# Starting the FFN's first pair of batches inside attention's last two tiles, and copying V of each batch's second tile without its wait on a DMA

## What is computed

```python
for i in range(DEPTH):            # DEPTH = 6
    x = attn_layer(shift_tokens(x), Wqkv[i], q_scale[i], k_scale[i], Wo[i]) + x
    x = ffn_layer(shift_tokens(x), ln_g[i], ln_b[i], W1[i], b1[i], W2[i], b2[i]) + x
```

```python
mu = x.mean(-1, keepdims=True)
var = ((x - mu) ** 2).mean(-1, keepdims=True)
xn = (x - mu) / jnp.sqrt(var + 1e-05) * g + bln
a, gate = jnp.split(xn @ W1 + b1, 2, -1)      # 341 channels each
return a * jax.nn.gelu(gate, approximate=False) @ W2 + b2
```

## Time and profile before

| | us |
|---|---|
| runs (three) | 4357.13, 4359.65, 4364.4 |
| median | 4359.65 |
| profiled execution, its own time | 4356.64 |
| its span, first to last instruction | 4354.8 |
| PE busy | 4059.5 (93%) |
| DVE busy | 3340.9 (77%) |
| ACT busy | 2354.2 (54%) |
| POOL busy | 2615.3 (60%) |
| mean granted TensorE clock | 0.978 |

### The profile page before, as it was taken

The page is one execution under the profiler, slowest core; times in us unless marked ns, Lnnn a source line. Parts: engine busy times, 40 slices in busy tenths (PEclk is TensorE's granted clock), DMA queues, the critical chain, the costliest instruction groups (busy, mean ns, idle before and its releaser), DMA issues. The chain is left out here.

```text
span 4354.8 us, 164452 instructions
## 1 busy us (share of the span) xinstructions
PE 4059.5 (93%) x68429; PEld 2650.8 (61%) x68429; DVE 3340.9 (77%) x5657; ACT 2354.2 (54%) x3362; POOL 2615.3 (60%) x3605
## 2 busy tenths in 40 slices
PE   4988999979998999998999999999899998999998
PEld 2554333346776667765677666776657776577765
DVE  7786988758787687876878767788767877688776
ACT  3664777745554455554555544555445555455553
POOL 5462111067875478772787736878457785477871
PEclk9998999989999999999999999999999999999999
DMA  2222111133232132321323213233123322133221
GB/s 76 85 81 67 56 52 54 35 84 81 76 82 66 44 81 74 82 68 42 80 77 84 76 31 82 75 83 79 51 59 80 83 76 71 39 78 82 76 74 40
DMA packets 218146, 300.55 MB, mean 69 GB/s; under 512 B 44336, under 2 KB 112048, under 8 KB 216624
## 3 DMA queue, kind: packets, MB, share of 16 engines
q1 hardware_dynamic: 217520, 290.63, 24.9%
HBM read 60.29 MB, written 14.68 MB: 17 GB/s over the span
## 5 line engine op out<-in xcount | busy, mean ns | idle before, releaser
L1586 ACT ACTIVATE ls_r<-PS 128x1024 f32<-128x1024 f32 x192 | 196.7, 1025 | 768.5 <-PE PS L1416 742.2
L1723 DVE TENSOR_REDUCE ls_ss<-ls_r 128x16 f32<-128x1024 f32 x384 | 465.9, 1215 | 83.9 <-ACT ls_r L1624 83.9
L1713 DVE TENSOR_TENSOR ls_a<-PS,TC 128x1024 f32<-128x1024 f32 x384 | 467.8, 1220 | 65.6 <-ACT ls_r L1586 60.1
L1293 POOL TENSOR_TENSOR ls_a<-ls_a,ls_q 128x1024 f32<-128x1024 f32 x192 | 453.9, 2364 | 92.8 <-DVE ls_q L1718 91.8
L1718 DVE TENSOR_TENSOR ls_q<-PS,TS 128x512 f32<-128x512 f32 x768 | 491.6, 682 | 0.0
L1316 POOL TENSOR_TENSOR ls_a<-ls_a,ls_q 128x1024 f32<-128x1024 f32 x192 | 456.8, 2379 | 2.6 <-DVE ls_a L1713 2.6
L1624 ACT ACTIVATE ls_r<-PS 128x1024 f32<-128x1024 f32 x186 | 190.8, 1026 | 390.1 <-PE PS L1481 390.1
L1481 PE MATMUL PS<-WQ,ls_xsT 128*128 128x512 f32 x744 | 386.5, 644 | 12.9 <-ACT ls_vt L1616 12.9
L1507 PE MATMUL PS<-WO,ls_r 128*128 128x128 f32 x3072 | 396.7, 283 | 0.8 <-ACT ls_r L1628 0.8
L1313 POOL TENSOR_TENSOR ls_a<-ls_a,ls_rn 128x1024 f32<-128x1024 f32 x192 | 365.4, 1903 | 29.2 <-DVE ls_rn L1783 14.6
L1318 POOL TENSOR_TENSOR ls_a<-ls_a,ls_rn 128x1024 f32<-128x1024 f32 x192 | 365.6, 1904 | 15.1
(11 more groups left out here) (281 smaller groups left out, 8473.4 us busy)
## 6 DMA issues: line engine op xcount, KB each, us to landing
ls_vb<-ls_vt SPq DMA_DIRECT2D x1152, 130.0 KB
ls_vb<-ls_vt SPq DMA_DIRECT2D x672, 65.0 KB
QT<-scratch SPq DMA_DIRECT2D x576, 32.0 KB
KT<-scratch SPq DMA_DIRECT2D x576, 32.0 KB
WQ<-wqkv SPq DMA_DIRECT2D x7, 1536.0 KB, 6.6
ls_xs<-XL SPq DMA_DIRECT2D x42, 256.0 KB, 3.4
ls_vb<-ls_vz SPq DMA_DIRECT2D x96, 65.0 KB
scratch<-QP SPq DMA_DIRECT2D x48, 128.0 KB, 1.8
```

Of the source, the lines that this page charges most:

```text
L1293: pool.tensor_tensor(a4[:, 1], a4[:, 1], b4[:, 1], ALU.add).then_inc(s_ck, 1)
L1713: nc.vector.tensor_tensor(v4(A[fq])[:, a], src, tab, ALU.mult).then_inc(done, 1)
L1723: nc.vector.tensor_reduce(ss[:, fq, a * H:a * H + H], v4(SQ)[:, a], AX.X, ALU.add).then_inc(done, 1)
```

## The change

Three things change, in each of the six layers.

1. The last two slots now have orders of their own: 4 is the second-last slot and 5 the last one. The rows of the first FFN pair are made one slot earlier, in the second-last slot. ACT now copies their lower channels too (DVE did). DVE centres stream 0 ahead of the reciprocals and stream 1 behind the scaling of the output; ACT squares both between the copy of transposed K and the copies of the transposed output.
2. The transposes of the first pair, its gain and bias, and four of its six gate products (chunks 1 and 2 of each stream) stand in the last slot; the first pair is taken out of the FFN loop.
3. ACT copies V of a batch's second tile (t = 1) without the wait for the windows of t = 0.

```diff
                 for j in range(NT):
-                    slot(*last(j), 3 if j < NT - 1 else 4)
+                    slot(*last(j), 3 if j < 2 else j + 2)
...
             def ahead(eng, layer):
-                with loop(eng, 0, PAIRS - 1) as p:
+                layer(0, True, True)
+                with loop(eng, 1, PAIRS - 1) as p:
                     layer(p, True)
                 layer(PAIRS - 1, False)
...
+                def rows_across(s, at, m):
+                    pe.wait_ge(f_xn[s], m)
+                    for t in range(NT):
+                        ins = pe.transpose(at[:, t * P:t * P + P], xs[s][:, t, :], ident)
+                    ins.then_inc(f_xt[s], 1)
+
+                def expand(s, part, c):
+                    k = P if c < DCH - 1 else DLAST
+                    at = part * DI + c * P
+                    return pe.matmul(bank(s, 1 + c)[0:k], WA[:, at:at + k], xsT[s][:, XO:], start=True, stop=True)
...
+                        if order == 5:
+                            for s in range(2):
+                                rows_across(s, banks(2 + s), l * PAIRS + 1)
+                            pe.wait_ge(f_xe[0], l * PAIRS + 1)
+                            pe.wait_ge(f_xe[1], l * PAIRS + 1)
+                            pe.wait_ge(w_ffn, l * 64 + 64)
+                            for c in range(1, DCH):
+                                expand(0, 1, c)
...
+                            if order == 5:
+                                expand(1, 1, 1)
                             pe.wait_ge(s_pte, 2 * n)
                             pe.wait_ge(s_vb[q], windows(l, b, t))
...
+                        if order == 5:
+                            expand(1, 1, 2)
                         if back:
                             pe.wait_ge(s_y, n)
...
-                                for c in range(DCH):
-                                    k = P if c < DCH - 1 else DLAST
-                                    at = part * DI + c * P
-                                    ins = pe.matmul(bank(s, 1 + c)[0:k], WA[:, at:at + k], xsT[s][:, XO:], start=True, stop=True)
+                                for c in range(1 if begun and part else DCH):
+                                    ins = expand(s, part, c)
...
-                        if order == 4:
-                            for a in range(2):
-                                act.wait_ge(f_sh[a], l * PAIRS + 1)
-                                act.activation(xs[a][:, :, D // 2:D], banks(2 + a)[:, 0:NT * D // 2].rearrange("p (t d) -> p t d", t=NT), ACT.Copy).then_inc(f_xu[a], 1)
+                        if order == 5:
+                            for s in range(2):
+                                affine(s, banks(2 + s), l * PAIRS + 1)
                         if back:
                             for c in range(2):
                                 half = PR[:, c * T:c * T + T]
                                 act.wait_ge(s_sub, 2 * n - 1 + c)
                                 act.activation(half, half, ACT.Exp).then_inc(s_ex, 1)
+                        if order == 4:
+                            for a in range(2):
+                                act.wait_ge(f_sh[a], l * PAIRS + 1)
+                                act.activation(xs[a][:, :, 0:D // 2], XL[:, a * PAIRS, 1:SLOTS, 0:D // 2], ACT.Copy)
+                                act.activation(xs[a][:, :, D // 2:D], banks(2 + a)[:, 0:NT * D // 2].rearrange("p (t d) -> p t d", t=NT), ACT.Copy).then_inc(f_xu[a], 1)
...
                         if front:
                             act.wait_ge(s_v, nf)
-                            if order > 1:
+                            if order > 1 and ft != 1:
                                 act.wait_ge(s_vb[1 - fq], windows(l, fb, ft - 1))
...
                         if order == 4:
-                            centred(0)
+                            kf[0] = 0
+                            zeroed(0, 0, 3)
...
                         if order == 4:
+                            zeroed(0, 1)
                             rooted(0)
                             scaled(0)
```

More of the change, by code:

```diff
@@ L1516, in ready, with layer @@
                             shift(s, 0, p + s * PAIRS, f_sh[s])
-                    def layer(p, more):
+                    def layer(p, more, begun=False):
                         m = l * PAIRS + p + 1
[L1520 to L1524, removed]
+                        for s in range(0 if begun else 2):
+                            rows_across(s, bank(s, 1), m)
                         if more:
@@ L1565, in _, with affine @@
                 with loop(act, 0, DEPTH) as l:
+                    def affine(s, src, m):
+                        act.wait_ge(w_ffn, l * 64 + 64)
+                        act.wait_ge(f_xt[s], m + 1)
+                        act.activation(xsT[s][:, XO:], src, ACT.Identity, scale=COL[:, 0:1], bias=COL[:, 1:2]).then_inc(f_xe[s], 1)
                     def prep(b):
@@ L1599, in slot @@
                                 act.activation(PRT[:, c * T:c * T + T], banks(PT_BANK[c]), ACT.Copy).then_inc(s_pte, 1)
[L1600 to L1604, removed]
                         if front and order == 1:
@@ L1620, in slot @@
                             act.activation(kT[:, :, k0:k0 + P], banks(KT_BANK, 2).rearrange("p (i n) -> p i n", n=P), ACT.Copy).then_inc(s_kte, 1)
+                        if order == 4:
+                            act.wait_ge(s_rdk, (l + 1) * TILES)
+                            for a in range(2):
+                                act.wait_ge(f_c[a], l * PAIRS + 1)
+                                act.activation(XQ[a], xs[a][:, :, :], ACT.Square).then_inc(f_sq[a], 1)
                         if front and order > 1:
@@ L1639, in uppers, with layer @@
                             act.activation(xs[s][:, :, D // 2:D], bank(s, 0)[:, 0:NT * D // 2].rearrange("p (t d) -> p t d", t=NT), ACT.Copy).then_inc(f_xu[s], 1)
-                    def layer(p, more):
+                    def layer(p, more, begun=False):
                         m = l * PAIRS + p + 1
[L1643 to L1646, removed]
-                            act.activation(xsT[s][:, XO:], bank(s, 1), ACT.Identity, scale=COL[:, 0:1], bias=COL[:, 1:2]).then_inc(f_xe[s], 1)
+                        for s in range(0 if begun else 2):
+                            affine(s, bank(s, 1), m)
                         if more:
@@ L1668, in _, with flink, zeroed @@
                     spread = lambda z: z.unsqueeze(2).to_broadcast([P, NT, D])
-                    def flink(p, ins):
-                        kf[0] += 1
-                        ins.then_inc(f_ch, 1)
+                    def flink(p, ins, n=1):
+                        kf[0] += n
+                        ins.then_inc(f_ch, n)
                         dve.wait_ge(f_ch, (l * PAIRS + p) * NF + kf[0])
+                    def zeroed(p, s, n=1):
+                        dve.wait_ge(f_xu[s], l * PAIRS + p + 1)
+                        flink(p, nc.vector.tensor_reduce(fs[:, 0, s, :], xs[s][:, :, :], AX.X, ALU.add), n)
+                        flink(p, nc.vector.tensor_scalar(fs[:, 0, s, :], fs[:, 0, s, :], -1.0 / D, None, ALU.mult))
+                        nc.vector.tensor_tensor(xs[s][:, :, :], xs[s][:, :, :], spread(fs[:, 0, s, :]), ALU.add).then_inc(f_c[s], 1)
                     def centred(p):
@@ L1681, in centred @@
                         for s in range(2):
-                            dve.wait_ge(f_xu[s], m)
-                            flink(p, nc.vector.tensor_reduce(fs[:, 0, s, :], xs[s][:, :, :], AX.X, ALU.add))
-                            flink(p, nc.vector.tensor_scalar(fs[:, 0, s, :], fs[:, 0, s, :], -1.0 / D, None, ALU.mult))
-                            nc.vector.tensor_tensor(xs[s][:, :, :], xs[s][:, :, :], spread(fs[:, 0, s, :]), ALU.add).then_inc(f_c[s], 1)
+                            zeroed(p, s)
                     def rooted(p):
```

## The result

| | before | after |
|---|---|---|
| median of the runs (12 each) | 4361.74 | 4353.28 |
| lowest to highest | 4356.41 to 4371.79 | 4343.91 to 4358.47 |
| profiled execution, its own time | 4356.64 | 4351.97 |
| its span | 4354.8 | 4350.1 |
| mean granted TensorE clock | 0.978 | 0.983 |

The ratio is 0.9979, 95% interval 0.9972 to 0.9987: 9.2 us faster, by the profiled executions 4.7. The forecast was 4340, range 4329 to 4351: the direction was right, the size was not.

A forecast was written before the change was run, and what follows sets the result against it. PE was busy 93% of the span, but at the changed places engines waited for one another. V -12.9 and six layers of -0.8 (slots +0.2, first pair -1.0) took 4356.64 to 4338.9, as median 4341.9; stated 4340, range 4329 to 4351.

The forecast's parts named there:

- V of the second tile: Second slot of each layer: without ACT's wait for windows the Q product starts earlier; 12.9 us gained, bounds 7.5 and 24.3.
- all of it moves forward: Behind the Q product: ACT's square, DVE and the next scores all start earlier; 2.02 us in the second layer.
- the Q product regains its rate: Rival, second slot: the Q product runs at full rate again, up to 11.4 us more, 4329; chance 0.12.
- The slots: Attention's last two slots together, maxima to last residual: 27.86 us against a mean of 27.68, costing 0.2 a layer.
- reciprocals to maxima: From the second-last slot's reciprocals to the last slot's maxima: 8.35 us, before 7.11.
- the last slot's: Last slot, from its maxima to its reciprocals: 7.15 us, before 6.96.
- The first pair: FFN's first pair: next transposes 17.1 us after the residual, not 18.08; gain 1.0 a layer.
- some 2 us: First pair: PE stands still this long ahead of its linear products, since GELU starts only at T + 4.0 (T: the residual).
- The rule on table loads: ACT's GELU table load takes 1.28 us; whatever follows lasts 0.89 at most, against the skill's 1.38 of draining.

The follow-up runs named there:

- v_only: The kernel before with only ACT's wait at the V copy removed for the second tile; 4343.86, ratio 0.9968.
- v_unrolled: v_only with DVE's first FFN pair written ahead of its loop, no engine doing other work; 4352.84, ratio 0.9987.
- dve_loop: The changed kernel with DVE's first FFN pair back in its loop; 4337.89, ratio 0.9950.
- pad_ahead: v_only with 56 one-column memsets on DVE between attention's last slot and the FFN loop; 4366.24, ratio 1.0011.
- ffn_loop: dve_loop with ACT's wait at the V copy put back; 4359.94, ratio 1.0002.
- ffn_only: The changed kernel with ACT's wait at the V copy put back; 4356.33, ratio 0.9994.
- gates_late: dve_loop with all gate products of the first pair put back into the FFN; 4345.74, ratio 0.9971.
- tail2_pad15: The changed kernel with DVE looping over the first two FFN pairs, the last two written out, and 15 small memsets behind the last pair; 4346.32, ratio 0.9965.
- pad_behind: v_only with the same 56 memsets on DVE, placed behind the FFN loop's last pair; 4350.4, ratio 0.9975.

## Why the prediction was wrong

**V of the second tile.** The step "all of it moves forward" was right about the path and wrong about what else the change does to it. The copy, transposed K and the Q product stand as forecast. The term of 12.9 was too small rather than too large: v_only's own execution is 13.9 shorter in span though its slots and FFN happened to be 0.3 a layer longer, and its start gives 3.37 a layer, not 2.15. Of the 12.9 us of waits the first layer has only 1.0, so the five starts have 2.37 each; the other 1.03 is the rate of the Q product (2.71 us for 3.74). So the rival "the Q product regains its rate" came true by about half of its 1.9 a layer, in v_only's second layer as far as POOL allows. In the changed kernel most of that is lost again: behind DVE's gap PE waits 3.48 us, and its Q product takes 3.15 in the second layer and 3.04 in the mean.

**The step that was missing.** Nowhere did I price that the first pair is taken out of DVE's loop too, though DVE does the same in it as before. This costs 21.58 - 19.26 = 2.3 us at each of five jumps, 11.6 in all, of the 13.1 by which the profiled execution (4351.97) missed its forecast of 4338.9. v_unrolled shows it without the FFN part, dve_loop the FFN part without it, and pad_ahead with no copied pair at all. dve_loop, at 4337.89, is where the forecast had put the changed kernel, but in part by luck: V gives more there than was forecast and the FFN part less, as the sum below shows.

**The slots** were forecast at +0.2 and are +0.35 (28.27 for 27.92). Of the single steps, reciprocals to maxima is 8.17 for 8.35, the last slot's 7.45 for 7.15. The cost was right, its reason too: the residual of DVE is last, and the next maxima at 1384.11 follow it on DVE without a wait.

**The first pair** was forecast at -1.0 and gave nothing, for two reasons. Where PE's clock holds, the next transposes come 17.55 (after) to 17.66 (dve_loop) behind the residual, not 17.1: DVE's product starts at 9.9 to 10.0, not 9.65, and the FFN is 74.3 against 74.73 in four layers before, a gain of 0.4. And in five of the six layers of after the linear products run slowly behind PE's wait of 1.90 us. The clock over them, after's first layer and dve_loop's:

```profile
1402.60:1409.80 7.20, 7.12 (x14) 2.92 (x15) 5.04 (x16) 1.75 (x4) 0.98 (x1) 0.76 0.44 88
```

```profile
1402.90:1408.40 5.50, 5.42 (x12) 2.05 (x12) 4.42 (x16) 1.73 (x4) 0.96 (x1) 1.00 0.55 111
```

That is 0.8 in each such layer. The prediction had this wait of PE ("some 2 us") but put no price on the clock behind it. The wait is the same in both, so it alone doesn't decide: the slow stretch was in five layers of six in after, in one of dve_loop, in three each of ffn_loop and ffn_only. But without the wait it never came: before, v_only and gates_late, where PE runs on, have a clock of 1.00 there in all layers. Two FFNs of the kernel before are 0.6 longer all the same, at full clock; the fifth layer's, columns as above:

```profile
3692.50:3704.50 12.00, 12.00 (x33) 5.45 (x31) 10.51 (x24) 7.95 (x12) 4.08 (x4) 1.00 0.62 180
```

So the FFN part made the stretch possible; what tips it in one layer and not in another stays open.

**Sum.** With the gap gone, by spans: starts -16.6, first start -1.0, slots +1.9, FFN -3.2, steady slots +0.1, together -18.8 for the forecast's -17.7. V's starts give 16.6 where the whole V term was 12.9; slots, first start and FFN together give 2.3 for 4.8. In after the gap adds 11.6 and the FFN, mostly by its slow stretches, 3.3; what is left of the 4.7 is the scatter of steady slots and first start.

**The rule on table loads.** The load ends at 1400.78 and GELU starts at 1400.79, so nothing passes behind a load; of the 0.89 that the earlier trace rows left open none belongs to it. The Trainium skill, page "ScalarE: Activation LUTs", section "What ACT_TABLE_LOAD costs", adds 1.38 us of draining to each load. It is not there: in all six layers GELU starts 0.01 us behind the load's end, and in the first the load itself stands 0.03 behind the copy before it.

## What to carry to other kernels

Taking an iteration out of a loop is an edit of every engine whose code it copies: do it on those engines alone that do something else in it, and look at each engine's jump for an idle time with "issue" behind it. Compare the packets of the instruction queues between two kernels; they show at once whose code no longer stays. A new gap costs nothing beside a longer wait, so remove waits and check for such gaps in one go, and price a removed wait, and a new one, with the clock it leaves behind, not by its length alone.

## What the runs showed of the hardware

- DVE's layer body, with two inner loops in it, was run through its five jumps without a fetch there with 395 executed instructions when each loop is counted once (tail2_pad15, `q14` at 42 packets), and was fetched anew each time (after, 67 packets; the 26 over before's are 0.21 MB, 8 KB each) with 381. The straight piece between its inner loops tells the cases apart: 107 to 112 instructions in the kernels without the gap, 163 to 169 in those with it. A limit between these fits all kernels here; it was not tried apart whether it is this piece's length, its place, or where the code falls on the borders of the fetched pieces.
- Where DVE's code was fetched at the jump, DVE stood idle for 2.5 to 2.8 us (twenty gaps in after, ffn_only, v_unrolled and pad_ahead). The Trainium skill, page "Runtime: NRT & Kernel Launch", section "Instruction fetch mechanics", says that a taken branch whose target is outside the two pages held forces such a fetch before execution goes on. The trace agrees that there is a stall with a fetch in it. Which code is held it doesn't show; the body's length alone doesn't decide it, as pad_ahead and pad_behind are equally long.
- A wait of PE of 1.90 us was followed by a stretch at the lower level of the clock in some layers and not in others (over the linear products the clock was 0.76 in after's first layer, 1.00 in dve_loop's). With four gate products in PE's waits of the last slot the clock there was 1.00 (dve_loop), without them 0.52 (gates_late), and 16 output products took 2.05 us for 3.78.
